# A transformer layer on one core: another order of the opening's stores, weight loads, projections and flag read

## The reference, cut to what matters

```
x = x + attention(layernorm(x)) @ out_w.T      # 16 heads of 16, rotary q and k
                                               # mask: j <= i and (same block of 64, or |i-j| <= 128, or j < 4 or i < 4)
h = silu(n @ w1.T * s1) * (n @ w2.T * s2)      # n = layernorm(x), 1024 wide
h = gelu(h @ h1.T * hs1)                       # exact gelu
h = gelu(h @ h2.T * hs2)
x = x + h @ w3.T * s3
```

## Time and profile before

| what | value |
|---|---|
| median of 3 runs | 1191.78 us (1191.38 to 1192.52) |
| profiled execution | 1194.19 us, its span 1192.3 us |
| mean granted TensorE clock | 0.971 of full speed |
| busy: PE, DVE, ACT, POOL | 1091.3, 649.3, 715.3, 472.2 us |
| DMA | 198.54 MB, mean 167 GB/s |

### The profile page before, as it was taken

One profiled execution on the slowest core, in us unless ns is written; L12 is line 12 of the kernel. 1 busy time (PEld: TensorE's weight loads), 2 busy tenths in 40 slices (PEclk: granted clock), 3 DMA queues, 4 the chain that ended last, 5 costly groups with the idle time before them and its releaser, 6 DMA issues.

```text
span 1192.3 us, 21621 instructions
## 1 busy us (share of the span) xinstructions
PE 1091.3 (92%) x7538; PEld 877.2 (74%) x7538; DVE 649.3 (54%) x1986; ACT 715.3 (60%) x1774; POOL 472.2 (40%) x656
## 2 busy tenths in 40 slices
PE   4175869999999999999999999999999999999998
PEld 2144667778867787778877788777877778778887
DVE  3078535754566545755566555765557554554422
ACT  1445545765666844855657745857657756866422
POOL 6243142722543433723535323634427223323433
PEclk9678989999999999999999999999999999999999
DMA  9777745776447344555537364465446464431540
GB/s 300 234 195 251 222 147 171 243 234 178 150 130 233 111 155 160 179 175 148 180 109 243 101 195 148 151 198 158 133 136 213 122 193 152 117 107 54 177 141 18
DMA packets 138269, 198.54 MB, mean 167 GB/s; under 512 B 7856, under 2 KB 90032, under 8 KB 138160
## 3 DMA queue, kind: packets, MB, share of 16 engines
q1 hardware_dynamic: 138160, 197.14, 53.8%
HBM read 155.16 MB, written 49.28 MB: 171 GB/s over the span
## 4 chain that ended last, share of the span: by engine, by line
PE 83%; SPq 4%; DVE 4%; DMA 3%; ACT 2%; issue 2%; POOL 1%; POOLq 0%; ACTq 0%; DVEq 0%
PE bank L708 39%; PE bank L679 10%; PE bank L732 5%; PE bank L618 5%; PE bank L575 5%; PE bank L587 4%; PE bank L516 4%; PE bank L595 3%; PE bank L540 2%; PE bank L641 2%; SPq L370 2%; SPq L330 1%; DMA qk_scratch<-split 1%; DMA Qs<-qk_scratch 1%; PE bank L631 1%
## 5 line engine op out<-in xcount | busy, mean ns | idle before, releaser
L851 ACT ACTIVATE Sm<-Sm,smin 128x260 f32<-128x260 f32 (+2 forms) x512 | 241.4, 473 | 211.4 <-DVE smin L1033 210.9
L708 PE MATMUL bank<-b_hi,W 128*128 128x512 f32 x512 | 216.5, 423 | 0.5 <-POOL b_lo L1284 0.5
L708 PE MATMUL bank<-a_hi,W 128*128 128x512 f32 x512 | 210.4, 411 | 1.1 <-DVE a_act L1120 1.1
L708 PE MATMUL bank<-b_lo,W 128*128 128x512 f32 x512 | 201.3, 393 | 0.0
L708 PE MATMUL bank<-a_lo,W 128*128 128x512 f32 x512 | 201.0, 392 | 0.0
L1084 DVE TENSOR_SCALAR a_sum<-bank,scales 128x512 f32<-128x512 f32 x64 | 48.0, 751 | 159.4 <-PE bank L708 159.4
L679 PE MATMUL bank<-x_hi,W 128*128 128x256 f32 x512 | 127.0, 289 | 7.6 <-issue 7.6
L1293 POOL TENSOR_TENSOR a_lo<-a_act,a_hi 128x256 fp32r<-128x256 f32 x128 | 94.2, 738 | 83.5 <-ACT a_hi L898 83.5
L679 PE MATMUL bank<-x_lo,W 128*128 128x256 f32 x512 | 125.4, 286 | 0.0
L575 PE MATMUL bank<-Ks,Qs 128*128 128x256 f32 (+1 forms) x512 | 100.3, 319 | 19.9 <-DVE a_act L1120 8.2
L1033 DVE CUSTOM_DVE_ANT_0 Sm<-bank,msk,gmin 128x256 f32<-128x256 f32 x256 | 108.4, 480 | 11.3 <-PE bank L575 11.3
(11 more groups left out here) (110 smaller groups left out, 2188.2 us busy)
## 6 DMA issues: line engine op xcount, KB each, us to landing
W<-w_scratch SPq DMA_DIRECT2D x168, 512.0 KB, 4.0
qk_scratch<-split SPq DMA_DIRECT2D x128, 256.0 KB
Qs<-qk_scratch SPq DMA_DIRECT2D x128, 128.0 KB, 4.7
Ks<-qk_scratch SPq DMA_DIRECT2D x16, 1024.0 KB, 8.5
w_scratch<-in_ffn_w SPq DMA_DIRECT2D x22, 512.0 KB, 8.1
stage_a<-in_ffn_w SPq DMA_DIRECT2D x16, 512.0 KB, 8.5
x_in<-in_x SPq DMA_DIRECT2D x8, 512.0 KB, 9.2
x<-in_x SPq DMA_DIRECT2D x8, 512.0 KB, 4.0
```

What stands on the lines that cost most here:

```text
L708: mm = nc.tensor.matmul(bank[n % 2][:, :], lhsT.bitcast(F32) if general else lhsT, rhs, start=(kk == 0 and part == 0), stop=(kk == NH - 1 ...
L851: ex = nc.scalar.activation(row, row, ACT.Exp, bias=smin[:, r, c:c + 1], scale=-1.0, accum_out=rowsum[:, i % 2, col:col + 1])
```

## The change

1. SP's opening issues no weights. After the mask come the stores of q and k of both halves, and each stack is loaded as soon as its stores have landed; out_w, scales and s3 follow. The mask has a semaphore of its own (msk_loaded), and attn_loaded counts the other three.
2. For sequence 0 the second half is split into a second buffer, split_first, that lies where PT is used later.
3. The weights are loaded by ACT's queue: h1 in two DMAs of 2 MB once x_in is in, in rows of 16 KB; the up weights (2 MB), the down weights (1 MB) and h2 (four of 1 MB) at steps 0 to 5 of round -1. ACT's checks 4, 5 and 6 move from ahead of round -1 to the ends of its steps 3, 4 and 5, and the last one from step 16 to step 13. POOL places four chunks in the opening and four at steps 4 to 7, cutting them out with strides. look_at_late moves one step on.
4. In round -1 all of the projections of sequence 1 stand three steps (SHIFT) later; bank 6 is used in the order OPENING there. SP's save_split stands at 9, 11, 12 and 13, load_x(2) at 12, saves of weights at 14 and 15. xn2 of tiles 0 and 1 is made by POOL at steps 14 and 15.
5. The four v products of sequence 1 go to banks 0 and 1, one at the end of each step from 16 to 19.
6. The flag is now `exact` (1 when there are no low bits), read behind step 15 (KNOWN = 16); steps 16 to 19 and the v products become part of both bodies. If runs rounds(False), Else rounds(True).
7. The gated tile s = 2 of round 0 waits for v_kept, since banks 0 and 1 hold v.

The diff, cut to its core:

```
+SHIFT, KNOWN = 3, UNITS
+OPENING = ("t0", "t1", "qk0", "qk1", "o0", "qk2", "qk3", "gs", "o1", "pg0", "o2", "n0", "pg1", "n1", "n2", "o3",
+           "vg", "n3")
...
+        split_first = sb("split_first", [P, 4, SEQ], F32R, at=pt_at)
...
+        def v_bank(b, t):
+            if b == 1:
+                return bank[t // 2][:, t % 2 * EMB:(t % 2 + 1) * EMB]
+            return bank[4 + t % 2][:, 0:EMB]
+
+        def parts_of(b, f):
+            return split_first if (b, f) == (0, 1) else split
...
-        N_CONST = 4
+        N_CONST = 3
...
-                    if r == -1:
-                        if n < SLOTS:
-                            stage_late(n)
-                        elif n < SLOTS + 4:
-                            save_weights(OTHERS[n - SLOTS])
...
-                    if has_q(r):
+                    if r >= 0 and has_q(r):
...
+                    if r == -1:
+
+                        if n in (9, 11, 12, 13):
+                            save_split(1, n // 12, int(n in (11, 13)))
+                        if n == 12:
+                            load_x(2)
+                        if n >= 14:
+                            save_weights(OTHERS[2 * n - 28])
+                            save_weights(OTHERS[2 * n - 27])
...
-            for j in range(SLOTS):
-                stage_weights(j)
-            sp.dma_start(msk[:, :, :], mask).then_inc(attn_loaded, 16)
+            sp.dma_start(msk[:, :, :], mask).then_inc(msk_loaded, 16)
+            for kind in range(2):
+                save_split(0, 0, kind)
+            save_split(0, 1, 0)
+            load_queries(0, 0, 0)
+            load_keys(0, 0)
+            save_split(0, 1, 1)
+            load_queries(0, 0, 1)
+            load_keys(0, 1)
...
-            for j in range(SLOTS, SLOTS + EARLY):
-                stage_weights(j)
-            for f in range(NF):
-                for kind in range(2):
-                    save_split(0, f, kind)
-            load_first_stacks(0)
...
+            for n in range(KNOWN):
+                if n == KNOWN - 1:
+                    pe.wait_ge(low_found, 1)
+                    nc.tensor.matmul(bank[0][0:1, 0:1], low_all[:, :], minus_half, start=True, stop=True)\
+                        .then_inc(low_added, 1)
+                step(-1, n, False)
             pe.wait_ge(low_ready, 1)
-            low_bits = pe.value_load(low_int[0:1, 0:1], min_val=0, max_val=1)
+            exact = pe.value_load(exact_int[0:1, 0:1], min_val=0, max_val=1)
...
+                beside_attention(-1, general, KNOWN)
...
-            with pe.If(low_bits):
+            with pe.If(exact):
+                rounds(False)
+            with pe.Else():
                 rounds(True)
-            with pe.Else():
-                rounds(False)
...
-                wait(act, split_saved[1 - f][kind], 16 * SAVES * (b + f))
-                nc.scalar.activation(split[:, 2 * kind, :], (q, k)[kind][:, f, :], ACT.Copy,
+                if (b, f) == (1, 0):
+                    act.wait_ge(split_saved[0][kind], 16 * SAVES)
+                elif b:
+                    act.wait_ge(split_saved[1 - f][kind], 16 * SAVES * (b + f))
+                nc.scalar.activation(parts_of(b, f)[:, 2 * kind, :], (q, k)[kind][:, f, :], ACT.Copy,
...
+            def stage_later(n):
+                if n == 0:
+                    act.dma_start(stage_b[:, 0:4, :].rearrange("p s c -> p (s c)"), ffn_w[:, W_UP:W_H1])\
+                        .then_inc(up_staged, 16)
+                if n == 1:
+                    act.dma_start(stage_b[:, 4:6, :].rearrange("p s c -> p (s c)"), ffn_w[:, W_DN:W_DN + 2 * SLOT])\
+                        .then_inc(dn_staged, 16)
+                if 2 <= n < 2 + NH // 2:
+
+                    j = n - 2
+                    if j == 0:
+                        act.wait_ge(low_summed, SLOTS // 2)
+                        act.wait_ge(w_placed, 4)
+                    act.dma_start(stage_a[:, 2 * j:2 * j + 2, :].rearrange("p s c -> p (s c)"),
+                                  ffn_w[:, W_H2 + 2 * j * SLOT:W_H2 + 2 * (j + 1) * SLOT]).then_inc(h2_staged[j], 16)
...
-                    if r == -1 and n == UNITS:
+                    if r == -1 and n in (3, 4, 5):
+                        check_weights(n + 1)
+                    if r == -1 and n == 13:
                         check_weights(CHECKS)
...
+            act.wait_ge(x_loaded, 16)
+            for n in range(2):
+                act.dma_start(stage_a[:, 4 * n:4 * n + 4, :].rearrange("p s c -> p (s c)"),
+                              ffn_w[:, W_H1 + 4 * n * SLOT:W_H1 + 4 * (n + 1) * SLOT]).then_inc(h1_staged[n], 16)
...
+                    nq = n if r >= 0 else n - SHIFT
+                    if r == -1 and n == 14:
+                        low_bits()
...
+                    if r == -1 and n == KNOWN - 1:
+                        no_low_bits()
```

More of the change, by code:

```diff
@@ L481, in misc_free @@
                 else:
-                    order = [u for u in ROUND if has_q(r) or u[0] in "opn"]
+                    order = [u for u in (ROUND if r >= 0 else OPENING) if has_q(r) or u[0] in "opn"]
                     n = order.index(name)
@@ L529, in global_scores, with v_projection @@
                 mm.then_inc(g_done, 1)
-            def v_projection(r):
+            def v_projection(r, tiles=range(NT)):
                 b = r + 2
-                for t in range(NT):
-                    if t < 2:
+                for t in tiles:
+                    if b == 1:
+                        if t == 0:
+                            pe.wait_ge(low_ready, 1)
+                    elif t < 2:
                         wait(pe, (prev_kept, cur_kept)[t], (LATER, UNITS)[t] * (b - 1))
@@ L774, in step, with beside_attention @@
                         ln2_transposes(r, n - UNITS)
-            def beside_attention(r, general):
-                for n in range(STEPS):
+            def beside_attention(r, general, first=0):
+                for n in range(first, STEPS):
                     step(r, n, general)
+                    if r == -1 and n >= UNITS:
+                        v_projection(r, [n - UNITS])
                 if has_q(r):
-                    v_projection(r)
+                    if r >= 0:
+                        v_projection(r)
                     values_of_first(r)
@@ L1047, in keep_cur @@
                 wait(dve, pv_done, UNITS * a + n - 1)
+                if a == 0 and n == 0:
+                    for kind in range(2):
+                        dve.wait_ge(split_saved[1][kind], 16 * SAVES)
                 nc.vector.tensor_copy(PT[:, n % 2, 1, :, :].rearrange("p c q -> p (c q)"), bank[5][:, :])\
@@ L1276, in place_weights @@
             def place_weights(slot):
-                pool.wait_ge(stage_loaded[slot // 2], 32)
-                nc.gpsimd.tensor_copy(W[:, slot, :], stage_a[:, slot, :]).then_inc(w_placed, 1)
+                if slot in UP_SLOTS:
+                    pool.wait_ge(up_staged, 16)
+                    j = UP_SLOTS.index(slot)
+                    src = stage_b[:, 0:4, j * 2 * P:(j + 1) * 2 * P]
+                else:
+                    for n in range(2):
+                        pool.wait_ge(h1_staged[n], 16)
+                    src = stage_a[:, :, slot * P:(slot + 1) * P]
+                nc.gpsimd.tensor_copy(W[:, slot, :].rearrange("p (k o) -> p k o", o=src.shape[2]), src).then_inc(w_placed, 1)
             def deep_lo(r, layer, part):
@@ L1339, in _ @@
             for slot in range(SLOTS):
-                place_weights(slot)
+                if slot not in UP_SLOTS:
+                    place_weights(slot)
             take_global_scores(0)
```

135 lines of the change are left out of this document (73 added, 62 removed).

## The result

The changed kernel is slower: 1199.21 us, median of 7 runs (1195.67 to 1200.23), against 1192.52 of the kernel before in the same session. The ratio is 1.0048, 95% interval [1.0038, 1.0059]; the two medians alone would give 1.0056. Forecast were 1181 us, with 1171 to 1189 as the range.

The account below looks back on a forecast made before the run. TensorE is nearly always busy from the first gated product (156.8 us); waits set the opening before it. Saving 8.8 us there plus 2.6 for the clock, less 0.5 at the end, gives 10.9: 1181 us, range 1171 to 1189.

Parts of the forecast that it names:

- three signs of being wrong: Query stacks release units 4 or 6 late, check 4 waits past 66 us, or the end grows over 1 us.
- The query loads: SyncE's query loads in mid attention: need 5.2 us, have three steps, nothing late in front of them.
- rival A: Query pair of unit 4 starved by ScalarE's large rows: lands at 71 us, 7 us lost, 1188 us; chance 0.13.
- The main case: The term-by-term forecast of 1181 us, own range 1174 to 1187; chance 0.62 together with an ineffective branch swap.
- The start of the units: Opening: stores from 21 us without gaps, first masked minimum at 54.0 instead of 60.4 us, bounds 50.5 and 58.
- Rotary to the end of step 15: VectorE's stretch from 77.5 us: 40.2 busy plus waits, sum 53.8, ending at 131.3 against 134.2 us.
- Rival B: Steps 9 to 13: a store group takes 15 us, not 9.3; 11.4 us lost, 1192, no change; chance 0.08.
- The flag: Stall at the flag's read and branch: 3.5 of 7.36 us saved, 3.8 left; bounds 0 and 6.
- Steps 16 to 19: Steps moved behind the flag stall: 12.9 us instead of 15.3, 2.4 saved, bounds 0 and 5.
- The clock: Gated products after the stall: 2.6 us saved when the clock recovers in steps 16 to 19 instead.
- The end: TensorE's jump over the Else body at the kernel's end: costs 0.5 us, bounds 0 and 4.
- Rival C: ScalarE's queue gets too little bandwidth, check 4's weights land near 78 us, 14.5 late: 1195 us; chance 0.10.

Follow-up runs that it names:

- rows2k: Changed kernel with the weights of steps 0 to 5 in 2 KB rows instead of 16 and 8 KB; 1192.18 us, ratio 0.9991 to the kernel before.
- saves_early: rows2k with SyncE's stores of sequence 1 at steps 8, 9, 11 and 12 instead of 9, 11, 12 and 13; 1185.02 us, ratio 0.9933.
- before_branch: Kernel before with only the two bodies of the branch exchanged, so the exact body follows the branch; 1189.17 us, ratio 0.996.
- branch_back: Changed kernel with the two bodies of the branch in their old order, nothing else; 1204.3 us, ratio 1.0101 to the kernel before.
- late_issue: saves_early with checks 4 to 6 in the opening, up and down weights issued behind ScalarE's copies of xnT in 2 KB rows; 1183.21 us, ratio 0.9914.
- early_big: saves_early with checks 4 to 6 in the opening, up and down weights behind the first 4 MB in 16 and 8 KB rows; 1182.5 us, ratio 0.991.
- late_issue_consts: late_issue with out_w, scales and s3 loaded ahead of the first stores; 1181.43 us, ratio 0.9898 to the kernel before.

## Why the prediction was wrong, point by point

Forecast span and measured span differ by 15.2 us (1181.4, 1196.6). The forecast named three signs of being wrong, and all three came: the pair of unit 4 was late, check 4 waited past 66 us (to 66.7, for 0.49 us only), and the end grew by 1.4 us. By the forecast's own steps:

- **The query loads (+7.2): rival A came true.** The main case gave them 5.2 us and three steps "with nothing late in front of them". They took 16.07: this is the largest step that failed, and rows2k and the row counts show why. The rival's working (15 us in the queues, 7 us lost, 1188 us) was right in mechanism and size, as rows2k shows (7.17 us, 0.57%). What failed is the sentence "Against: everything must move anyway", and so the chance of 0.13: total traffic says nothing on whose bytes go first. A further 1.5 us between first minimum and first rotary remain with small rows (25.1 us in rows2k, 23.5 forecast), where the pair still needs 8.9.
- **The start of the units (+4.2).** Stores from 21 us: right. "without a gap": wrong. Stores moved at 82 GB/s from 20 to 25 us and at 186 to 30, where the sum has 204 from the start: the k stores of the first half waited for their split until 24 us. So the second keys went out at 49.4, not 47.3. Then s3 took 7.2 us behind the second keys and out_w (1.25 MB). 58.2 us is just past the bound of 58.
- **Rotary to the end of step 15 (+3.3).** Term by term on VectorE: it was busy 41.2 us, not 40.2, since one look at late weights took 2.28 us and not 1.2. Its wait for the q split was 0.6, not 1.7, that for the k split 6.1, not 4.5. The wait for the flags was 3.2 as forecast. VectorE was ready for the k split 28.8 us after the rotary, as forecast (28.7), and the group of stores took 8.8 us, not 9.3. What failed is when the k stores are issued: 25.4 us after the rotary, not 23.3, since unit 11, behind which they stand, was scored 22.9 and not 21.3 us after it. It waited there for unit 10's minimum, behind VectorE's long look, and not for the first split, which came 0.4 us later (both in this trace, 113.31 and 113.76). The last term is the waits behind the k split (global keys and unit 12): 3.3 us, not 1.6, with the granted clock at 0.50 from 117 to 133 us. The other hand-offs came out as forecast. Rival B looked at this place but at the wrong term, the length of a group. That saves_early wins 7 us here is not the size of the error: the forecast had 7.8 us of these waits in its sum, and left them there.
- **The flag (-3.8).** Right in kind, mis-sized: I gave 3.5 us of 7.36 to the fetch. before_branch measures 6.2, branch_back 6.5. I left 3.8 us standing; before_branch keeps 1.1, and the changed kernel, which reads the flag in mid attention, keeps none.
- **Steps 16 to 19 (+0.6)**: 13.5 for 12.9 us. **The clock (+1.3)**: first gated product to last add shrank by 1.3 us (to 1031.6), not by 2.6. **The end (+0.9)**: it grew by 1.4 us, not 0.5.

Sum: 7.2 + 1.5 + 4.2 + 3.3 - 3.8 + 0.6 + 1.3 + 0.9 = 15.2.

**Rival C, the slower one,** did not happen as told: check 4 waited 0.49 us for its weights, at 66.7. That the time came out slower, as this rival has it, is no credit to it. The kernel is slower because A, the late start and the longer middle add up, each within or near a bound of its own, while the range was built as if only one of them could fail. Bounds on one side of one chain belong together.

**Where the gain went.** The stall at the flag brought 7.4 us (6.2 to 6.5 of them the fetch) less 1.4 at the end, steps 16 to 19 brought 1.8, the clock 1.3, the start of the units 2.2. The large rows cost 7 and the late stores 7; loads and checks in steps 0 to 5 cost some 2 more together (1.8 and 2.5 by the medians of saves_early against late_issue and early_big), which the runs do not part. With these mended the rest of the change is worth keeping: late_issue_consts is 0.6% faster than before_branch, whose whole gain is the branch.

**Not tried.** The shift of the projections by three steps was not undone by itself. With two steps the order in which bank 6 is handed on no longer fits, and would have had to be written anew. Why no row of the pair moves in its first 3 us is open too.

## What to carry to other kernels

Before moving loads to a second queue, list the small transfers on the first that something waits for, and give the second queue small rows or another time: total bandwidth does not protect them. But look at what small rows cost to issue, and put that issue where its engine has nothing to do. Put the body of a branch that is always taken right behind the branch. When several steps feed one chain, let the range hold two or three of their bad ends at once, and work out when each engine is ready, not only how long a transfer lasts.

## What the runs showed of the hardware that was not expected

- A DMA issue can hold the issuing engine for long: 10.90 us for four issues with 1536 rows of 2 KB behind 256 rows of 16 KB, 0.91 us for the same 3 MB in 256 large rows. The Trainium skill, page "DMA: Bandwidth & Descriptors", section "Issuing engines are not separate DMA queues", calls the time that an issue takes on its sequencer usually small beside the transfer; here 10.90 us of it put the start 10 us back.
- 512 rows of 512 bytes took 16.07 us beside rows of 16 and 8 KB, 8.88 beside rows of 2 KB, 5.2 (median) with no second queue at work. Once both queues moved rows there, each moved as many as the other, whatever their size: 540 and 540 in 11 us, or 407 and 415 in 3 us.
- The fetch of a distant body cost 6.2 to 6.5 us in the middle; at the end, where the last store ran beside it, the jump cost 1.4 to 1.9 us.
